# Two transformer blocks on one core: maxima split as columns and turned as bf16, block 1's sums and two lower parts of q and k on ScalarE and GpSimd

## The reference, cut to what matters

```python
def block0(x, c, ...):                       # x: 8 x 512 x 512, 16 heads of 32
    xn  = adaln(x, c, g1, w_ada1, b_ada1)
    qkv = bitlinear(xn, w_qkv, b_qkv)        # rows rounded to 8 bits, ternary weights
    attn = softmax(einsum('bhqd,bhkd->bhqk', q, k) * hd ** -0.5)
    x = x + bitlinear(einsum('bhqk,bhkd->bhqd', attn, v), w_proj, b_proj)
    h = gelu(bitlinear(adaln(x, c, g2, w_ada2, b_ada2), w_fc1, b_fc1))
    return x + bitlinear(h, w_fc2, b_fc2)

def block1(x, cond, ...):                    # one head of 512
    h = film(rmsnorm(x, norm1_w), cond, film1_w, film1_b)
    attn = softmax(einsum('bnd,bmd->bnm', h @ q_w + q_b, h @ k_w + k_b) * D ** -0.5)
    x = x + (einsum('bnm,bmd->bnd', attn, h @ v_w + v_b) @ proj_w + proj_b)
    h = film(rmsnorm(x, norm2_w), cond, film2_w, film2_b)
    return x + (gelu(h @ mlp_w1 + mlp_b1) @ mlp_w2 + mlp_b2)

out = block1(block0(x, cond), cond)
```

## Time and profile before

| what | value |
|---|---|
| median of 3 runs | 2288.89 us (2284.70 to 2292.79) |
| the profiled execution | 2284.53 us |
| its span, first to last instruction | 2282.7 us |
| mean granted clock of TensorE | 0.958 of 2.4 GHz |
| instructions on PE, DVE, ACT, POOL | 13491, 2821, 2082, 661 |

### The profile page before, as it was taken

One profiled execution on the slowest core, in us unless ns is written; L12 is line 12 of the kernel. 1 busy time (PEld: TensorE's weight loads), 2 busy tenths in 40 slices (PEclk: granted clock), 3 DMA queues, 4 the chain that ended last, 5 costly groups with the idle time before them and its releaser, 6 DMA issues.

```text
span 2282.7 us, 40192 instructions
## 1 busy us (share of the span) xinstructions
PE 2029.6 (89%) x13491; PEld 1019.2 (45%) x13491; DVE 1581.3 (69%) x2821; ACT 1149.2 (50%) x2082; POOL 722.1 (32%) x661
## 2 busy tenths in 40 slices
PE   3867787989998999899988999899989999899889
PEld 3345333444444444444445444444445444444434
DVE  5678636887578756886588757886588757885422
ACT  4365544564448444555447444655457443754230
POOL 1153233442126402541135302622145212731121
PEclk8788898999999999899999999999999999999989
DMA  6632452212230213111230213121230223011212
GB/s 225 207 103 100 159 187 88 86 39 84 88 103 25 102 60 126 48 57 65 94 106 18 101 71 125 39 84 56 85 112 20 86 91 116 25 57 56 93 37 92
DMA packets 85523, 200.82 MB, mean 88 GB/s; under 512 B 7612, under 2 KB 48864, under 8 KB 73144
## 3 DMA queue, kind: packets, MB, share of 16 engines
q1 hardware_dynamic: 74920, 166.49, 21.7%
q10 hardware_dynamic: 10384, 31.49, 3.8%
HBM read 161.97 MB, written 35.72 MB: 87 GB/s over the span
## 4 chain that ended last, share of the span: by engine, by line
PE 55%; issue 17%; DVE 14%; ACT 7%; POOL 5%; DMA 1%; DVEq 0%; ACTq 0%; POOLq 0%; SPq 0%
PE banks L1368 11%; PE banks L1370 10%; PE banks L1369 10%; PE banks L1326 5%; PE banks L1261 4%; POOL memory L1193 3%; DVE memory L1144 3%; PE banks L1138 2%; PE banks L1047 2%; DVE memory L961 2%; PE banks L1208 2%; PE banks L1182 2%; PE banks L1243 1%; PE banks L1312 1%; DVE memory L976 1%
## 5 line engine op out<-in xcount | busy, mean ns | idle before, releaser
L1368 PE MATMUL banks<-memory 128*128 128x512 bf16 x1536 | 589.5, 384 | 32.3 <-DVE memory L1616 11.8
L1369 PE MATMUL banks<-memory 128*128 128x512 bf16 x1536 | 584.7, 381 | 0.0
L1370 PE MATMUL banks<-memory 128*128 128x512 bf16 x1536 | 584.6, 381 | 0.0
L1193 POOL TENSOR_TENSOR memory<-memory 128x512 bf16<-128x512 f32 x288 | 324.4, 1146 | 317.3 <-ACT memory L1189 316.0
L1144 DVE TENSOR_REDUCE memory<-banks 128x1 f32<-128x512 f32 x512 | 333.6, 680 | 47.0 <-PE banks L1138 44.4
L1189 ACT ACTIVATE memory<-banks 128x512 f32<-128x512 f32 x512 | 290.3, 596 | 138.9 <-PE banks L1182 137.6
L1594 POOL TENSOR_TENSOR memory<-memory 128x512 bf16<-128x512 f32 x128 | 144.6, 1132 | 583.3 <-DVE memory L1589 583.3
L1368 PEld LDWEIGHTS banks<-memory 128*128 128x128 bf16 x1536 | 149.3, 97 | 220.2 <-DVE memory L1616 19.3
L1138 PE MATMUL banks<-memory 96*128 96x512 bf16 x512 | 198.5, 411 | 52.9 <-DVE memory L1144 46.9
L1370 PEld LDWEIGHTS banks<-memory 128*128 128x128 bf16 x1536 | 148.9, 97 | 187.5 <-issue 5.6
L1369 PEld LDWEIGHTS banks<-memory 128*128 128x128 bf16 x1536 | 152.3, 99 | 165.6 <-issue 5.0
(11 more groups left out here) (175 smaller groups left out, 2880.3 us busy)
## 6 DMA issues: line engine op xcount, KB each, us to landing
memory<-weight_parts SPq DMA_DIRECT2D x80, 1024.0 KB, 4.9
memory<-head_parts SPq DMA_DIRECT2D x192, 128.0 KB, 2.8
head_parts<-memory SPq DMA_DIRECT2D x64, 256.0 KB, 2.8
weight_parts<-memory ACTq DMA_DIRECT2D x10, 1024.0 KB, 4.9
memory<-in_x SPq DMA_DIRECT2D x32, 256.0 KB, 3.3
memory<-ada_rows SPq DMA_DIRECT2D x16, 512.0 KB, 4.5
memory<-in_L_cond_w_fc ACTq DMA_DIRECT2D x2, 4096.0 KB, 14.2
memory<-in_L_cond_mlp_w ACTq DMA_DIRECT2D x8, 1024.0 KB, 8.4
```

Of the source, the lines that this page charges most:

```text
L1193: eng.tensor_tensor(prob_lo[:, e % RING], expo[:, e % RING], prob_hi[:, e % RING], ALU.subtract).then_inc(ok.sem, 1)
L1368: pe.matmul(bank, lh, rh, start=(k == 0), stop=False)
L1369: pe.matmul(bank, lh, rl, start=False, stop=False)
L1370: mm = pe.matmul(bank, ll, rh, start=False, stop=(k == KC - 1))
```

## The change

1. **Maxima.** Once a group's maxima stand, DVE cuts the 16 columns into a bf16 part and a bf16 rest (`cut_maxima`: one cast, one subtraction, both 128x16). PE turns eight bf16 pieces 128x4, into one bank read as bf16; ACT copies both rows in one instruction of 1024 elements (`copy_maxima`); SP sends two rows. `max_high` and `max_low` go. The slots are (0,15), (1,7), (2,7), (3,7) on DVE, and (0,18), (1,9), (2,9), (3,9) on PE and ACT.
2. **Block 1's sums.** `proj_scale1` (ACT, new) reads the bank and scales into `y1`; `proj_add1` is now a plain addition on POOL, t = 0 to 2 ahead of the first `prob_low`, t = 3 ahead of that of e = 6. `squares1` waits for it. `invert1` moves ahead of `p_low`.
3. **Two low parts.** For q and k of group 2 ACT repeats the bias addition in fp32 in place, and POOL subtracts (`qk_rest`), in place of `qk_low` on DVE.
4. **Slots.** e = 42 goes from DVE to POOL (`FIRST_DVE` 43); on DVE and ACT the reading of the transposed probabilities is one slot later; q2's product and high part and k2's high part, the squares and `turn_y1` move by one or two slots.

The core of the diff, without what repeats it:

```diff
-LATE_QK = {(0, 6): ("q", 2), (0, 12): ("k", 2), (1, 3): ("q", 3), (1, 6): ("k", 3)}
+LATE_QK = {(0, 5): ('q', 2), (0, 12): ('k', 2), (1, 3): ('q', 3), (1, 6): ('k', 3)}
-LATE_HIGH = {(0, 5): ('q', 2), (0, 9): ('k', 2), (1, 4): ('q', 3), (1, 9): ('k', 3)}
+LATE_HIGH = {(0, 4): ('q', 2), (0, 11): ('k', 2), (1, 4): ('q', 3), (1, 9): ('k', 3)}
-FIRST_DVE = 42
+FIRST_DVE = 43
-TURN_AT = ((2, 7), (2, 9), (2, 11), (2, 13))
+TURN_AT = ((2, 6), (2, 8), (2, 10), (2, 12))
-SQUARE_AT = ((1, 4), (1, 6), (1, 8), (1, 10))
-PT_AT, PT_READ = (((0, 3), (0, 10), (0, 15)), ((0, 2), (0, 11), (0, 14)))
+SQUARE_AT = ((1, 4), (1, 5), (1, 7), (1, 9))
+PT_AT, PT_READ = (((0, 3), (0, 10), (0, 15)), ((0, 3), (0, 12), (0, 15)))
-MAX_AT = {(0, 17): 0, (1, 8): 1, (2, 11): 2, (3, 10): 3}
-HIGH_AT = {(0, 17): 0, (1, 9): 1, (2, 10): 2, (3, 9): 3}
-LOW_AT = {(0, 17): 0, (1, 11): 1, (2, 11): 2, (3, 12): 3}
+MAX_AT = {(0, 18): 0, (1, 9): 1, (2, 9): 2, (3, 9): 3}
+HIGH_AT = {(0, 18): 0, (1, 9): 1, (2, 9): 2, (3, 9): 3}
+LOW_AT = {(0, 15): 0, (1, 7): 1, (2, 7): 2, (3, 7): 3}
+POOL_AT = (0, 0, 0, 6)
+QK_POOL = (("q", 2), ("k", 2))
...
+                if (name, c) in QK_POOL:
+                    act.wait_ge(hi_ok.sem, hi_ok(i, 2 * c + a + 1))
+                    act.activation(qk_f[:, a], qk_f[:, a], ACT.Identity, bias=bias).then_inc(qk_sum.sem, 1)
+
+        def qk_rest(pool, i, c, part):
...
+            pool.tensor_tensor(part_lo[:, a], qk_f[:, a], part_hi[:, a], ALU.subtract).then_inc(lo_ok.sem, 1)
...
+        def cut_maxima(dve, i, c):
...
+            whole = neg_max[:, c % 2].rearrange("p t j -> p (t j)")
+            dve.tensor_copy(max_cols[:, 0], whole).then_inc(max_cut.sem, 1)
+            dve.wait_ge(max_cut.sem, max_cut(i, 2 * c + 1))
+            dve.tensor_tensor(max_cols[:, 1], whole, max_cols[:, 0], ALU.subtract).then_inc(max_cut.sem, 1)
+
         def turn_maxima(pe, i, c):
-            done(pe, plan0, ("s", c, HEADS - 1), i)
+            pe.wait_ge(max_cut.sem, max_cut(i, 2 * c + 2))
             b = take(pe, plan0, ("max", c), i)
-            for t in range(TT):
-                mm = pe.transpose(banks[0:G, b, t * P:(t + 1) * P], neg_max[:, c % 2, t], ident)
+            out = banks[0:G, b].bitcast(BF16).rearrange("p (s t n) -> p s t n", s=2, t=TT)
+            for s in range(2):
+                for t in range(TT):
+                    mm = pe.transpose(out[:, s, t], max_cols[:, s, t * G:(t + 1) * G], ident_bf)
             mm.then_inc(full[b].sem, 1)
 
-        def max_high(act, i, c):
+        def copy_maxima(act, i, c):
...
-            act.activation(max_hi[0:G], banks[0:G, b], ACT.Copy).then_inc(max_parts.sem, 1)
...
+            act.activation(max_rows[0:G].rearrange("p s n -> p (s n)"), banks[0:G, b].bitcast(BF16), ACT.Copy
+                           ).then_inc(free[b].sem, 1)
...
-        def proj_add1(dve, i, t):
...
-            dve.scalar_tensor_tensor(out=x1[:, t], in0=banks[:, b], scalar=suminv1[:, t:t + 1],
-                                     in1=x1[:, t], op0=ALU.mult, op1=ALU.add).then_inc(free[b].sem, 1)
+        def proj_scale1(act, i, t):
+            b = ready(act, plan1, ("proj", t), i)
+            act.wait_ge(inv1.sem, inv1(i, t + 1))
+            act.wait_ge(out_done.sem, out_done(i, 0))
+            act.activation(y1[:, t], banks[:, b], ACT.Copy, scale=suminv1[:, t:t + 1]).then_inc(free[b].sem, 1)
+
+        def proj_add1(pool, i, t):
+            done(pool, plan1, ("proj", t), i)
+            pool.wait_ge(x1_bias.sem, x1_bias(i, t + 1))
+            pool.tensor_tensor(x1[:, t], x1[:, t], y1[:, t], ALU.add).then_inc(x1_sum.sem, 1)
```

More of the change, by code:

```diff
@@ L130 @@
 SPLIT_LOW_AT = (7, 16, 17, 18, 19, 20, 21, 22)
-MAX_AT = {(0, 17): 0, (1, 8): 1, (2, 11): 2, (3, 10): 3}
-HIGH_AT = {(0, 17): 0, (1, 9): 1, (2, 10): 2, (3, 9): 3}
-LOW_AT = {(0, 17): 0, (1, 11): 1, (2, 11): 2, (3, 12): 3}
+MAX_AT = {(0, 18): 0, (1, 9): 1, (2, 9): 2, (3, 9): 3}
[3 more added lines that the diff above has]
+QK_POOL = (("q", 2), ("k", 2))
 EXTRA_DVE = (17, 22, 25, 30, 34, 38)
-LOW_DVE = [e for e in range(KC * HEADS) if e >= FIRST_DVE or e in EXTRA_DVE]
+EXTRA_POOL = ()
+LOW_DVE = [e for e in range(KC * HEADS) if (e >= FIRST_DVE or e in EXTRA_DVE) and e not in EXTRA_POOL]
 LOW_POOL = [e for e in range(KC * HEADS) if e not in LOW_DVE]
@@ L290, in two_blocks @@
         ada = fp32(2, D)
-        max_hi, max_lo = bf16(T), bf16(T)
+        max_rows = bf16(2, T)
+        max_cols = bf16(2, HEADS)
         ring_at = top[0]
@@ L1734, in both @@
                         residual_bias0(pool, i, 0, t)
-                    for t in range(TT):
+                if i is not None:
+                    for t in range(2):
                         value_low(pool, i, t)
+                if i is not None:
+                    for t in range(2, TT):
+                        value_low(pool, i, t)
+                    for part, late in QK_POOL[0:1]:
+                        qk_rest(pool, i, late, part)
+                if i is not None:
+                    for part, late in QK_POOL[1:2]:
+                        qk_rest(pool, i, late, part)
                 for c in range(KC):
@@ L1739, in both @@
                         e = c * HEADS + n
+                        if j is not None:
+                            for t, at in enumerate(POOL_AT):
+                                if e == at:
+                                    proj_add1(pool, j, t)
                         if i is not None and e in LOW_POOL:
@@ L1777, in highs1 @@
                             p_high(act, j, *at)
+                        elif name == "proj":
+                            proj_scale1(act, j, *at)
                         elif name == "fc1":
@@ L2027, in both @@
                             part, late = LATE_LOW[c, n]
-                            qk_low(dve, i, late, part)
+                            if (part, late) not in QK_POOL:
+                                qk_low(dve, i, late, part)
                         if (c, n) in LOW_AT:
-                            max_low(dve, i, LOW_AT[c, n])
+                            cut_maxima(dve, i, LOW_AT[c, n])
                         e = (c - 1) * HEADS + n - 1
```

51 lines of the change are left out of this document (24 added, 27 removed).

## The result

The change is slower: 2303.27 us median (2296.77 to 2309.46, 7 runs) against 2285.06 for the kernel before (2283.20 to 2292.79, 7 runs), a ratio of 1.0069, 95% interval 1.0049 to 1.0089: some 16 us by the ratio, 18 by the medians. The forecast was 2275.7 and the range ended at 2292. The profiled execution took 2304.55 us, its span 2302.7, its clock 0.958, as before.

A forecast was written before the change was run, and what follows sets the result against it. VectorE was taken to hold TensorE up in block 0's attention. Seven passes gave -13.3 us, ramp -1, tail +1.1: -13.2 us, 2271.3 for the profiled execution, 2275.7 as median; range 2258 to 2292.

The forecast's parts named there:

- the cut's price: VectorE's four cuts per pass: 0.5 us each, between two small pointwise instructions and two whole rows (1.2), plus a wait.
- (0,x) and (1,x) together: First two slot stretches of block 0's attention: 1.75 us better per pass by (2,3), capped by GpSimd, not VectorE.
- GpSimd becomes the bound: Rival: GpSimd's lows slow to 1.29 us, e15 ends 2.7 us later, +19 over seven passes, 2308 us; chance 0.09.
- point of decision: The time per GpSimd low, 1.2 us, from which the rival of GpSimd as the bound was to decide.
- e15: Last of GpSimd's sixteen lows in slots (1,x): ended at 699.95 before, forecast 698.2, or 702.6 at 1.29 us per low.
- Slots (0,x): First stretch of block 0's attention: projection 0.3 us later, turning +0.15, VectorE waits -1.28; -0.8 us in an undisturbed pass.
- The ramp: Before the seven steady passes: VectorE also serves ternarisation and loses lows and `max_low`; 0 to -3 us, taken -1.
- The tail: After the last pass, no scores hide the sums: 0.75 becomes 0.6+1.1 us plus a handover, +1.1.
- the 0.6 us wait for bank 5: TensorE's wait in slots (1,x), bank held by `qk_scale`: claimed to go with the `proj_add1` at (1,5).
- The sums: Four `proj_add1` leave VectorE: 3.5 of about 6 us less VectorE work per pass.
- the working of (1,x): Second stretch: VectorE alone would allow 1.6 to 2.4 us less; GpSimd's lows and norm operations end at 698.2, capping it.
- The clock rival: Slow passes clear, another 9 us, 2267, chance 0.17; or all passes fall, +9, 2285, within a shared 0.24.

The follow-up runs named there:

- Run 5: The change, with the cut of the maxima made by three VectorE reductions in place of a cast and a subtraction: 2297.17 us, ratio 1.0055.
- run 16: The change, with TensorE turning the truncated upper halves of the fp32 maxima without waiting and two reductions making the rest: 2280.42 us, ratio 0.9975.
- run 14: The kernel before with only the slots of the turning and of ScalarE's high part set as in the change: 2273.01 us, ratio 0.9941.
- Run 1: The change without its maxima part: fp32 turning, low part out of the bank, old slots: 2281.88 us, ratio 0.9990.
- run 3: The kernel before with block 1's sums alone moved to ScalarE and GpSimd, with the slots that go with them: 2293.44 us, ratio 1.0042.
- run 18: The kernel before with the new turning slots and q2's and k2's lower parts moved, block 1's sums left on VectorE: 2275.87 us, ratio 0.9953.
- run 13: The change with the old maxima method at the new turning slots, and old FiLM slots and first low of VectorE's tail: 2270.97 us, ratio 0.9936.
- run 17: The kernel of run 16 with the FiLM slots and the first low of VectorE's tail as before: 2288.23 us, ratio 0.9999.

## Why the prediction was wrong

1. **The step that failed is the cut's price.** "It costs no more than two whole rows (1.2) and no less than two pointwise ones of 0.21; I take 0.5". It measured 0.37, 1.67, 0.80 and 1.13 us for the four groups of a pass, 4.0 in place of 2.0; the upper bound did not hold. The bound looked at size, and size was not the price. A row of before had the right one: VectorE's own `prob_low`, the same kind of instruction among the same GpSimd work (ns: least, median, most):

```profile
L1193 DVE TENSOR_TENSOR memory<-memory x224: 669/682/1525, 156.7 to 2005.7; 128x512 bf16<-128x512 f32 x112
```

   682 and 1525: the second is the first plus most of a GpSimd low. `max_low`, which the cut replaces, read a bank and held 0.67. "`max_low` becomes a cut (-0.1)" exchanged a form that GpSimd cannot hold for two that it can.
2. **What waits on it.** The working had (0,x) and (1,x) together better by 1.75 us. It priced the cut as VectorE's work and put TensorE's wait for it at nothing, without a reason. This term is the larger: the wait at (1,9) went from 0.59 to 1.65 us and the clock behind it from 1.00 and 0.91 to 0.81. Run 5 removes the cut's stretch alone and gets back 3 to 6 us (by the ratios, by the medians), run 16 the wait too and gets back some 22.
3. **The rival that named the cause was dismissed.** "GpSimd becomes the bound" got 0.09, because "most of VectorE's work in (1,x) reads a bank". The mechanism was half right: GpSimd's lows did not grow (1.15 and 1.13 us in the mean), and TensorE, which waited 1.3 us for them over the run before, has no such wait after; it was VectorE that they held. Its point of decision was set at 1.2 us per low (by its own sum e15 is late from 1.12 on); the lows of e0 to e15 took 1.09 in the mean and the loss came all the same. They began at 679.57, as worked out (679.6), and ended at 700.60 in place of 698.2, 1.5 us of it in waits for ScalarE.
4. **Slots (0,x)** were right: -0.8 forecast, -0.5 at the first score by key and -0.9 at head 0 measured.
5. **The ramp**: -1 forecast between 0 and -3; the first score of the second batch starts 2.6 us earlier (394.42 for 397.06). **The tail**: +1.1 forecast, +1.2 measured for the sums. The add takes 1.27 us, not 1.1, and the square starts 2.06 us behind the scaling's start, where it started 0.84 behind the add's. ScalarE before, then after:

```profile
2182.84 0.63 ACT L1380 ACTIVATE memory<-memory 128x512 f32<-128x512 f32 x1 [1.88 <-DVE memory L1564]
```

```profile
2199.66 0.69 ACT L1585 ACTIVATE memory<-banks,memory 128x512 f32<-128x512 f32 x1 [1.30 <-PE banks L1390]
...
2201.72 0.63 ACT L1401 ACTIVATE memory<-memory 128x512 f32<-128x512 f32 x1 [0.16 <-POOL memory L1590]
```

6. **A term was missing.** The turning moves from (0,17) to (0,18), (1,8) to (1,9), (2,11) to (2,9) and (3,10) to (3,9). The prediction gave it no price; run 14 puts some 13 us of gain on it. The forecast's size, -13, would have been reached by these two lines alone, and that is chance. The working let the 0.6 us wait for bank 5 go with the add at (1,5). Run 1, without that add on VectorE, still has it (0.73 us at the same place); run 14, with the add, does not.
7. **The sums** were held for the main relief. Alone they cost 9 us (run 3): the norm's wait of 1.63 us behind GpSimd, which the working of (1,x) did not follow past GpSimd's lows, though this wait stood in the trace of before at 0.76 us already. With the new slots they are worth nothing that shows (runs 14, 18 and 13).
8. **The clock rival** held a fall "in every pass" possible, in (0,x). In the change it fell in every pass, but behind the second turning: (0,x) is at 1.00 in all of them. Over the six full passes TensorE spends 61 us at the 1.2 GHz level, before 48 (0 to 13.7 in a pass, 10.2 in each of the change). Before, a pass with 13.7 us of it takes 2.5 us more than one with none, so by an estimate from these numbers the difference is worth 0.4 us of the 3 a pass lost. The waits are the rest.

Two things stay open. Why the new slots gain is settled in part: the wait for bank 5 goes, 4.9 us over the run, and 13 is what the medians show. Run 14's profiled execution was the slowest of its five and still 6.1 us faster than that of before; 2.4 of them fall ahead of the second batch's first score, and its passes (252.0 us on average, 252.5 before) are hardly shorter. And why the FiLM slots gain in run 13 and lose in run 17; passes of one program differ by 4 us with the clock (run 5: 252.1 to 256.4), so small shifts can decide such a thing, but that was only argued.
